# Another place for TensorE's jump back in the loop over the middle batches

## The reference, cut to what matters

```python
def reference(x, w_qkv, w_out, b_out, w_gate, w_up, w_down):   # x: (8, 1024, 512)
    xn = _layernorm(x, axis=-1)
    return x + _L0_attn_ref(xn, w_qkv, w_out, b_out) + _L0_ffn_ref(xn, w_gate, w_up, w_down)

def _L0_attn_ref(x, w_qkv, w_out, b_out):
    qkv = x @ w_qkv
    starts = jnp.arange(0, L - 4 + 1, 2)                # windows of 4 tokens, stride 2
    idx = starts[:, None] + jnp.arange(4)[None, :]
    q, k, v = jnp.split(qkv[:, idx], 3, axis=-1)        # 8 heads of 64
    ...
    attn = jax.nn.softmax(dots, axis=-1)
    o = jnp.einsum('bnhqk,bnkhd->bnqhd', attn, v)
    y = o.reshape(B, N, KS, C) @ w_out + b_out
    return jnp.zeros((B, L, C)).at[:, idx.reshape(-1), :].add(y.reshape(B, N * KS, C))

def _L0_ffn_ref(x, w_gate, w_up, w_down):               # fp4-rounded linear layers
    h = jax.nn.silu(fp4_linear(x, w_gate)) * fp4_linear(x, w_up)
    return fp4_linear(h, w_down)
```

## Time and profile before

| | |
|---|---|
| median of 3 runs | 2278.43 us (2278.31 to 2281.01) |
| profiled execution, its own time | 2275.91 us |
| its span, first to last instruction | 2274.1 us |
| mean granted clock of TensorE | 0.988 |
| PE busy | 2160.4 us, 95% of the span |
| DVE, POOL, ACT busy | 1638.1, 1220.4, 655.9 us |
| end of attention, start of feed_forward | about 893 us |

### The profile page before, as it was taken

How to read it: one execution, slowest core, us unless ns; L and a number is a source line. 1 busy time by engine, 2 the same in 40 slices (tenths; PEclk the granted TensorE clock), 3 DMA queues, 4 the chain that set the end, 5 groups by cost and what they waited for, 6 DMA issues and landing times.

```text
span 2274.1 us, 46572 instructions
## 1 busy us (share of the span) xinstructions
PE 2160.4 (95%) x16704; PEld 1041.8 (46%) x16704; DVE 1638.1 (72%) x3097; ACT 655.9 (29%) x1007; POOL 1220.4 (54%) x880
## 2 busy tenths in 40 slices
PE   1899999999999987999999999999999999999998
PEld 0454444444444443444444444444444444444443
DVE  5587667666767555787787778778778777777774
ACT  1233334243333322222222222222222322222221
POOL 2166566566756444555555555555555555555552
PEclk9999999999999998999999999999999999999999
DMA  7547565664647427333333333433333333333332
GB/s 231 162 106 184 122 176 143 158 154 131 177 114 184 118 89 222 63 85 84 81 84 84 87 85 79 91 81 84 84 81 84 84 84 83 82 82 83 84 73 66
DMA packets 447373, 251.81 MB, mean 111 GB/s; under 512 B 365251, under 2 KB 371907, under 8 KB 447253
## 3 DMA queue, kind: packets, MB, share of 16 engines
q1 hardware_dynamic: 445860, 244.88, 43.9%
q10 hardware_dynamic: 1104, 4.19, 0.5%
q0 software_dynamic: 288, 0.94, 0.1%
HBM read 98.98 MB, written 59.77 MB: 70 GB/s over the span
## 4 chain that ended last, share of the span: by engine, by line
PE 59%; DVE 1%; POOL 0%; DMA 0%; issue 0%; POOLq 0%; ACT 0%; SPq 0%; DVEq 0%
PE dn L1235 13%; PE gu L1220 7%; PE gu L1224 7%; PE gu L1225 7%; PE gu L1222 7%; PE gu L1221 7%; PE gu L1223 7%; PE dn L1237 6%; POOL hv L169 0%; DMA ht<-hh 0%; DVE hv L205 0%; DVE hv L203 0%; POOLq L989 0%; DVE hv L1116 0%; DVE hs L179 0%
## 5 line engine op out<-in xcount | busy, mean ns | idle before, releaser
L904 PE MATMUL acc<-late 128*128 128x512 f16 x2304 | 527.8, 386 | 79.3 <-DMA late<-xh 56.0
L1235 PE MATMUL dn<-late,ht 128*128 128x512 f16 x1408 | 429.9, 380 | 5.3 <-DMA ht<-hh 5.3
L904 PEld LDWEIGHTS acc<-late 128*128 128x128 f16 x2304 | 221.4, 99 | 351.6 <-issue 99.7
L1116 DVE SCALAR_TENSOR_TENSOR hv<-gu,row_gains,sg 128x512 f32<-128x512 f32 (+1 forms) x192 | 129.0, 672 | 279.0 <-ACT sg L1180 279.0
L169 POOL TENSOR_TENSOR hv<-hv,hs 128x1408 f32<-128x1408 f32 x64 | 165.8, 2590 | 230.0 <-DVE hv L205 230.0
L1220 PE MATMUL gu<-late,turned 128*128 128x512 f16 (+1 forms) x768 | 277.9, 362 | 7.3 <-PEq L223 6.9
L1221 PE MATMUL gu<-late,turned 128*128 128x512 f16 (+1 forms) x768 | 277.8, 362 | 0.0
L1223 PE MATMUL gu<-late,turned 128*128 128x512 f16 (+1 forms) x768 | 277.8, 362 | 0.0
L1224 PE MATMUL gu<-late,turned 128*128 128x512 f16 (+1 forms) x768 | 277.8, 362 | 0.0
L1225 PE MATMUL gu<-late,turned 128*128 128x512 f16 (+1 forms) x768 | 277.8, 362 | 0.0
L1222 PE MATMUL gu<-late,turned 128*128 128x512 f16 (+1 forms) x768 | 277.8, 362 | 0.0
(11 more groups left out here) (124 smaller groups left out, 3258.7 us busy)
## 6 DMA issues: line engine op xcount, KB each, us to landing
late<-in_L_attn_x SPq DMA_DIRECT2D x64, 256.0 KB, 3.6
normed<-late SPq DMA_DIRECT2D x64, 256.0 KB, 2.4
res<-in_L_attn_x SPq DMA_DIRECT2D x64, 256.0 KB, 2.9
attended<-res SPq DMA_DIRECT2D x64, 256.0 KB, 2.5
raw<-normed SPq DMA_DIRECT2D x64, 256.0 KB, 2.7
pr<-attended SPq DMA_DIRECT2D x64, 256.0 KB, 2.7
out<-fo SPq DMA_DIRECT2D x64, 256.0 KB, 2.0
ready<-turned SPq DMA_DIRECT2D x36, 256.0 KB, 2.3
```

The source lines that it names most:

```text
L904: last = pe.matmul(out, lhsT, rhs, start=(at == 0), stop=(at == n - 1))
L1235: last = pe.matmul(dps[k][:, :], ht[:, k, at], w_hi, start=(at == 0), stop=(at == 2 * FC - 1))
```

## The change

The two strings of TensorE are cut at another place. Before, `first` ended with `p7'` (the last output projection of the batch before), and the loop began with `v6`. Now `first` goes on up to `q4+`, and the loop begins with `q5+`. The cycle of groups and their order stay the same, and so does every wait. The steps `v6 s2 W1+ v7 a2 q0+ q1+ q2+ a3 q3+ q4+` are now unrolled once ahead of the loop instead of behind it. (`W1+` makes instructions for the first batch only.)

```diff
             batches(pe,
-                    "p6' v4 s1 a0 v5 a1 p7'",
-                    "v6 s2 W1+ v7 a2 q0+ q1+ q2+ a3 q3+ q4+ q5+ a4 q6+ q7+ v0+ p0 a5 v1+ s0+ p1 a6 v2+ p2 a7 v3+ q8+ "
+                    "p6' v4 s1 a0 v5 a1 p7' v6 s2 W1+ v7 a2 q0+ q1+ q2+ a3 q3+ q4+",
+                    "q5+ a4 q6+ q7+ v0+ p0 a5 v1+ s0+ p1 a6 v2+ p2 a7 v3+ q8+ "
                     "q9+ q10+ q11+ p3 q12+ q13+ p4 a8 q14+ p5 W2+ q15+",
```

## The result

The changed kernel takes 2256.91 us (median of 4 runs, 2254.3 to 2260.72) against 2278.37 us: a ratio of 0.9907, with a 95% interval of 0.9895 to 0.992. It is faster by 0.9%, 21 us. The forecast was 2252 us, in a range of 2244 to 2265. The profiled execution took 2254.3 us (span 2252.5), 21.6 us less than that of before.

A forecast was written before the change was run, and what follows sets the result against it. TensorE (PE), busy 95% of the span, was taken as the bound. Winning 34.0 us of jump cost, less 5 x 1.0 for new jumps and 2.5 of waits, gave 26.5 us: 2252 us, range 2244 to 2265.

The forecast's parts named there:

- The five old jumps: TensorE's five attention-loop jumps between p7' and s2 cost 34.0 us in all, which the change can win.
- The branch: At the new jump ahead of q5: about 4.1 us, covered by 3.9 us of queued matmuls, leaving 0.8 us idle.
- The second stall: Stall shortly behind the jump's target, where its instruction block ends: shrinks to 0 to 0.5 us, taken as 0.2.
- All five new jumps: Jumps between q4+ and q5+ cost 1.0 us each, 5.0 us in all.
- The clock: TensorE around the jumps: no half clock after 0.8 + 0.2 us idle; otherwise 2.2 us a jump.
- What comes back from other engines: PE waits for other engines in the loop: 0.5 us a pass, 2.5 us in all, bounds 0 and 8 us.
- The waits for a3's weights: Weights made by POOL and DVE could be late at a3; slack of 7.4 us loses 5.8, keeps 1.6.
- It adds no matmul and no wait: Premise for TensorE's order: only the jump and its target's block move; no size given.
- the queue did not cover all: Rival: TensorE's queue holds more than 18 matmuls and hides the branch at the new jump; 2248 us, chance 0.08.
- the waits did not come back by microseconds: Rival: DVE or SP late by 3 to 4 us a pass at q8 or a3; 2265 us, chance 0.10.
- Rival 3: New jump's target again near its block's end, so second stall and half clock return; about 2278 us, chance 0.06.
- Rival 4: New jump waits for a next-block fetch under way, costing 8.34 us each with half clock; 2288 us, chance 0.04.

The follow-up runs named there:

- The run behind s2: Changed kernel with TensorE's jump moved to between the score group s2 and v7, after small matmuls: 2276.7 us, ratio 0.9994.
- both reverse edits: Idle instructions at TensorE's start: ten in the kernel before, 2265.95 us; 73 in the changed kernel, 2291.57 us.
- the run with 73: Changed kernel with 73 idle instructions at TensorE's start: 2291.57 us, ratio 1.0062.
- at the old place with ten instructions: Kernel before, jump still behind p7', with ten idle instructions at TensorE's start: 2265.95 us, ratio 0.9949.
- at the old place with 44: Kernel before, jump still behind p7', with 44 idle instructions at TensorE's start: 2259.1 us, ratio 0.9917.
- fillers of 20 and 44: Changed kernel with 20 or 44 idle instructions at TensorE's start: 2256.1 us and 2253.0 us.
- 240: Changed kernel with 240 idle instructions at TensorE's start: 2277.7 us, ratio 0.9997.
- The moved loads: SP issues the edge-window loads of e3 and e4 later: changed kernel 2251.8 us, kernel before 2279.1 us; with e2 later and 44 idle instructions, changed kernel 2252.3 us.

## Why the prediction was right, and where its sizes were off

The account goes by the starts of TensorE's groups in the two profiled executions; forecast in brackets.

- **The five old jumps: 34.0 us won (34.0).** The difference between the traces grows by 8.34, 6.48, 6.28, 6.19 and 6.71 us from p7' to s2, each term of the forecast.
- **The branch.** 4.07, 4.16, 4.02, 3.88 and 3.41 us (4.1), and the lead of 3.9 us covered it but for 0.63, 0.71, 0.57, 0.51 and 0 us of gap (0.8). The run behind s2 shows what the cover is worth: without it 3.7 to 4.0 us.
- **The second stall.** None (0 to 0.5, taken as 0.2). The cause was forecast rightly, and both reverse edits show it: ten instructions take the stall away at the old place, 73 bring it back at the new. The Trainium skill's 256 instructions a block (Runtime: NRT & Kernel Launch, Instruction fetch mechanics) agree with the run with 73, which by that size has 5 left behind its target. **All five new jumps cost 3.2 us (5.0).**
- **The clock.** 1.00 through the loop, as taken. With single gaps of 1.6 to 2.6 us, at the old place with ten instructions, it stayed up as well; the half clock of before came with two gaps close together. A single gap does not always spare it: at the old place with 44 one of five gaps of 1.8 to 2.3 us, that of 2.07 us, was followed by a clock of 0.50 for 3.4 us and a v6 of 4.21 us.
- **What comes back from other engines.** PE's waits for DVE, ACT and the transposed rows in the loop were 1.9 us before and are 2.2 us now: 0.3 us (2.5). The waits for a3's weights did not come, and q8 waited 0.4 to 0.6 us in four passes.
- **The score groups: 7.2 us lost (not in the forecast).** This is the step that failed. "It adds no matmul and no wait" was true, and the time of the groups in between was taken as unchanged. Over six passes s2 went from 1.96 to 2.71 us, 4.5 us, and s0 from 1.88 to 2.38 us, 3.0 us; s1 gave back 0.3. s2 is shown to be slow because it now runs while SP issues e3 and e4. s0 has an end of a block at 38 instead of 29 instructions; fillers of 20 and 44 bring it to 1.7 us, 240 to 4.6 us, so its sensitivity to the blocks is shown. That these nine instructions explain all of its 0.5 us is argued from that.
- **The rest.** The changed kernel was 0.9 us ahead before the loop's stretch began (the loads at the start), and lost 1.5 us behind the last pass, mostly at the change of stages; about 1.1 us are in small pieces, none over 0.3 us. -34.0 + 3.2 + 0.3 + 7.2 - 0.9 + 1.5 + 1.1 = -21.6.

That the time fell so near the forecast is in part luck. The score groups cost 7.2 us that no term had, and the rest 1.7 us. The jumps came out 1.8 us and the waits 2.2 us better than taken, so that 5 us of error were left, within the range.

The rivals: the queue did not cover all, and the waits did not come back by microseconds. The Trainium skill's queue depth of 64 (TensorE: Matmul & The Clock Gate, the table at its head), taken as 32 pairs, would have left no gap; the gaps of 0.5 to 0.7 us speak for 18 pairs. Rival 3 needs the target near the end of its block, and the run with 73 shows its cost. Rival 4 needs a fetch under way at the branch that makes it wait; the runs at the old place show the fetch with branches of 4.3 to 5.3 us, but the run behind s2 shows it with branches of 3.6 to 4.0 us. As an account of the 5.44 us of the first branch it is therefore not shown.

What stays open: why the loads `ve<-v` that SP issues hold up TensorE's small matmuls, what makes some branches long, and why s1 with an end of a block at 42 is less hit than s0 at 54.

## What to carry to other kernels

A jump back of a long loop costs the fetch of its target less what is queued ahead of it, so it belongs behind the longest run of queued big matmuls, not behind small ones; its target wants more than 3 us of work left in its block of instructions (the next block came 3.3 us behind the first matmul here). Look at the DMA load and at the packets of the instruction queue around it as well. Count the instructions: here ten idle ones in front of the loop won 12 us and 44 won 19, where the move won 21. Groups of very small matmuls can stall on the supply of instructions, so look at where blocks end in them and what the DMA-issuing engine does meanwhile, also when the edit is elsewhere.

## What the runs showed of the hardware that was not expected

- A score group of 192 small matmuls takes 1.62 us at best and up to 5.4 us with the same waits met; unrolling the loop made 16 of 24 stop, for 33.3 us, and made the kernel slower than with five jumps of 6.8 us.
- Loads `ve<-v` issued by SP make a score group slow. In the changed kernel's two profiles the groups with four or five DMA issues in them, most of these such loads, take 2.2 to 3.0 us, against the 1.63 us of a group with none. The moved loads are the proof. That 30 of the 31 steps of 140 to 260 ns from one matmul to the next begin within 0.35 us of an issue says little: 83% of the time of these groups lies that near to one.
- The same branch takes 3.3 to 4.3 us in most jumps and up to 5.4 us in others; a packet of the next block within 1.0 us of it goes with 4.3 to 5.3 us at the old place with 10 and 44, and with 3.6 to 4.0 us behind s2.
- Ten or 44 idle instructions at the start of the program, where they cost nothing, took some 12 and 19 us off the kernel before.
